# First layernorm: the second batch's tiles are split in rows and turned by DMA transposes

## The chip, the cores and the metric

The kernel runs on one core of one Trainium2 chip. The time is that of the whole program on the device, in microseconds (us). A core has five engines, each with its own instruction queue: TensorE (PE, matrix products), VectorE (DVE), ScalarE (ACT), GpSimd (POOL) and SyncE (SP). SP computes nothing here; it issues every DMA of this kernel. Work on different engines is ordered by semaphores alone: an instruction waits until a counter has reached a value, and everything behind it on the same engine waits with it.

## The reference

One decoder layer on x of 2 batches x 512 rows x 1024 columns, in float32:

```
x = x + attention(layernorm(x))      # 32 query heads, 8 key/value heads of 128, causal
x = x + fake_quant(layernorm(x)) @ fake_quant(ctx)
x = x + gated_ffn(layernorm(x))      # 64 experts of rank 8, the best 16

# the head of attention(h), with h = layernorm(x):
q  = h @ Wq.T                        # 4096 columns
kc = h @ Wk_down.T ; vc = h @ Wv_down.T      # 256 columns each: the latents
k, v = (split of [kc, vc]) @ Wk_up.T, Wv_up.T
```

The change is in the first layernorm, at the very start, and in the latents' product behind it.

## The kernel before, in words

Every float32 operand of a product is split in two float16 parts, a high part (ACT rounds it) and a low part (DVE takes the rest, line 1188), and a product is three passes: high x high, high x low, low x high (line 1672).

The 1024 rows of x are eight tiles of 128 rows: tiles 0 to 3 are batch 0, tiles 4 to 7 are batch 1. `QT` is 4 and `TT` is 8. For each tile the opening does this:

- DVE takes mean and variance (line 1196), POOL a power (line 677), DVE the scale and the bias (lines 1210 to 1218), in `ln_stats` and `ln1_rstd`.
- ACT writes the normed rows, float32, to `hn`, which lies in the tensor `prob` (line 890, `ln1_apply`). `hn` has two places; tile t takes place t % 2.
- PE turns the tile, since the products need the columns of x on the partitions: eight 128x128 float32 transposes into two PSUM banks (line 1686, `columns`).
- ACT writes the high part from PSUM (`columns_hi`, two instructions of 128x512), DVE the low part (`columns_lo`, two instructions), into `h_block(b, j)`: the right factors of the query products, for batch b and half j of the columns. Three of these four blocks lie in `h_b`. The fourth, batch 1 and half 0, lies in `wo_in`.

Semaphores here: `ln_done` counts tiles normed, `ln_turned` half tiles turned, `ht_hi` and `ht_lo` split instructions of ACT and DVE.

The latents' product follows in four pairs of tiles ("pair" in the code: pair 0 is tiles 0 and 1, up to pair 3 with tiles 6 and 7). Each pair has four parts hp = 0 to 3, of 24 matmuls 128x256 each, 96 in all. PE's order puts the turning of tiles 2 to 7 between these parts, one tile ahead of the first two parts of pairs 0, 1 and 2. A pair waits for the low parts of its tiles. After pair 1 (batch 0) and pair 3 (batch 1) the latents go through ACT (line 882) and DVE (line 1240) into `lat`, which lies in `o_t`. Then PE computes keys and values of seven key/value heads (`kv_products`), 30 matmuls for each head and batch, whose results ACT and DVE split and SP stores to memory (`kv_parts`).

Beside this, POOL forms sums of the blocks (`part_sums`, line 701), four chunks of ten instructions on `q_tmp`, for the fast scheme of the query products. Its first chunk starts when all eight tiles are split. ACT and DVE take these sums out of `q_tmp` (`t_split`) behind the second head's keys and values, and POOL starts a second chunk only then.

SP's queue at the start is: loads of x and of weights, the first chunk of the context (`load_chunk`), then the loop with the loads of `up` weights (line 601, each waits for `up_lo`) and the stores of keys and values (line 607). Elsewhere in the kernel SP already issues DMA transposes: `turn` for the attention weights (128x1280, lines 554 and 557), and at the end `turn_h3` (128x1024, lines 636 and 638) and `turn_gated` (128x512, lines 644 and 646).

Of the kernel before, what the change touches and what calls it, by code (L numbers as in the profile page):

```python
# [8 lines left out]
F16 = mybir.dt.float16  # L9
BF16 = mybir.dt.bfloat16  # L10

P = 128
BATCH, SEQ, DIM = 2, 512, 1024
TOK = BATCH * SEQ
TT = TOK // P
# [181 lines left out]
    return LAST_WO + 2 * WO_STEP + max(c for c in range(WO_CHUNKS) if PAIR1_BANK[c % 8] == bank) + 1  # L197


def kind_of(g):  # L200
    if not isinstance(g, int):
        return "mid"
    return {0: "first", KV_HEADS - 1: "last"}.get(g, "mid")
# [7 lines left out]
def decoder_layer(nc, x, ctx_in, wq, wdown, wup, wo, a_w, b_w, router_w, keys, quant, ctx_whole, b_whole, kv_whole, out):  # L211
# [8 lines left out]
    with ctx:  # L220
# [74 lines left out]
              v_sb[:, :, :, :, :].rearrange("p a b c d -> p (a b c d)").bitcast(F32))  # L295
        h3_t = wq_sb[:, :, :, :].rearrange("p a b c -> p (a b c)").rearrange("p (t m n) -> p t m n", t=2, m=2)
        gated = q_tmp[:, 0, :]
        h3_s = wo_in[:, :, :].rearrange("p a b -> p (a b)").bitcast(F16).rearrange("p (t m n) -> p t m n", t=2, m=2)
        z_s = prob_s[:, :, 0:2 * HALF].rearrange("p t (m n) -> p t m n", m=2)
        column_term = wq_in[:, :, :].rearrange("p a b -> p (a b)").rearrange("p (b n) -> p b n", b=BATCH)  # L300
# [50 lines left out]
        o_lo = sem("o_lo")  # L351

        ht_hi = sem("ht_hi")
        wq_hi = sem("wq_hi")
        wo_hi = sem("wo_hi")
        up_hi = sem("up_hi")
# [83 lines left out]
        def _(sp):  # L440
# [154 lines left out]
                        load_ctx(0)  # L595

            load_chunk(0, 0)
            for n in range(KV_HEADS - 1):
                if n + 3 < KV_HEADS:
                    sp.wait_ge(up_lo, n + 1)  # L600
                    sp.dma_start(up_in[:, n % 3, :], wup[KV_ORDER[n + 3]]).then_inc(up_loaded[n % 3], 16)
                if n == 4:
                    for place in range(4):
                        sp.wait_ge(wq_lo, place + 1)
                        load_wq(place, 2 + place // 2)
                sp.wait_ge(gen_read, 2 * DOWN + 4 * (n + 1))
                sp.dma_start(kv_whole[KV_ORDER[n]], kv_stage[:, n % 2, :, :, :].rearrange("p a b c -> p (a b c)"))\
                    .then_inc(kv_stored[n % 2], 16)
# [54 lines left out]
        def _(pool):  # L663
# [36 lines left out]
                    at = q_tmp[:, place, :]  # L700
                    nc.gpsimd.tensor_tensor(at, at if left_ is None else left_, right, op).then_inc(t_op, 1)

            pool.wait_ge(ht_lo, 2 * TT)
            for n in range(KT // 2):
                part_sums(n)

# [98 lines left out]
        def _(act):  # L805
# [63 lines left out]


            def columns_hi(t):
                for j in range(2):
                    act.wait_ge(ln_turned, 2 * t + j + 1)
                    split_hi(h_block(t // QT, j)[:, 0, :, t % QT * P:(t % QT + 1) * P],
                             ps[:, 2 * (t % 2) + j, :].rearrange("p (k n) -> p k n", k=4), ht_hi, S_H)
# [7 lines left out]
                ins.then_inc(gen_hi, 1)  # L883

            def ln1_apply(t):
                if t >= 2:

                    act.wait_ge(ln_turned, 2 * (t - 1))
                act.wait_ge(rstd_done, t + 1)
                nc.scalar.activation(hn[:, t % 2, :], x_sb[:, t, :], ACT.Identity, bias=ln_bias[:, t:t + 1],  # L890
                                     scale=rstd1[:, 2, t:t + 1]).then_inc(ln_done, 1)
# [287 lines left out]
        def _(dve):  # L1179
# [47 lines left out]
            nc.vector.tensor_copy(ident_b[:, :], ident[:, :]).then_inc(newton, 1)  # L1227
            newtons[0] += 1
            def columns_lo(t):
                for j in range(2):  # L1230
                    dve.wait_ge(ht_hi, 2 * t + j + 1)
                    hi, lo = (h_block(t // QT, j)[:, part, :, t % QT * P:(t % QT + 1) * P] for part in range(2))
                    split_lo(lo, ps[:, 2 * (t % 2) + j, :].rearrange("p (k n) -> p k n", k=4), hi, ht_lo, S_H)
# [430 lines left out]
        def _(pe):  # L1664
# [27 lines left out]
            for pair in range(PAIRS):  # L1692
# [1 line left out]
                b, part = pair // 2, pair % 2  # L1694
                at = part * 2 * P
                for hp in range(DOWN):
                    if hp < 2 and 2 * pair + 2 + hp < TT:
                        columns(2 * pair + 2 + hp)
                    if hp == 0:
                        pe.wait_ge(ht_lo, 4 * (pair + 1))  # L1700
                    if pair == 0:
                        pe.wait_ge(wo_lo, hp + 1)
                    if b == 1 and part == 0:
# [31 lines left out]
                    pe.wait_ge(gen_read, max(kv_before(v), 2 * DOWN if b == 1 else DOWN))  # L1735
                    (k_product if kind == "k" else v_product)(n, b, kv_bank(v)).then_inc(gen_done, 1)

            pe.wait_ge(ht_lo, 2 * TT)
            for n in range(KV_HEADS - 1):
                kv_products(n)  # L1740
            for n in range(PLAIN_Q):
# [323 lines left out]
```

## Time and profile before

| | |
|---|---|
| time, median of 3 runs | 1109.15 us (1106.42 to 1109.94) |
| the profiled execution: time, span | 1110.08 us, 1108.3 us |
| granted TensorE clock, mean | 0.989 of full |
| PE busy | 1064.9 us, 96% of the span |
| DVE busy | 905.2 us, 82% |
| ACT busy | 530.3 us, 48% |
| POOL busy | 411.6 us, 37% |
| chain that ended last | PE 85%, DVE 8%, ACT 3%, issue 2%, DMA 1%, POOL 1% |
| DMA transposes in the program | 162, all issued by SP |

The span counts from the first to the last instruction, and the execution's own time is 1.8 us more. "Busy" counts an engine's instructions; it doesn't tell on what the end depends. The chain of waits does: it goes back from the last instruction to what released each step. In the row of the granted clock 1.00 is TensorE's full clock (2.4 GHz) and 0.50 the half (1.2 GHz).

### The profile page before, as it was taken

Reading aid. Unit: us, or ns where it says so; the run is one execution under the profiler, and the core shown is the slowest. Engines: PE = TensorE matmul, PEld = TensorE weight load, DVE = VectorE, ACT = ScalarE, POOL = GpSimd, SP = SyncE. Lnnn points to the kernel's source line nnn. Section 1 sums busy time; section 2 is a strip of 40 time slices with the busy share of each in tenths; the row PEclk is TensorE's granted clock in tenths of the full one; section 3 lists DMA queues with packets and bytes.
Section 4 is the critical chain, followed back from the end, with each engine's and each line's share of the span. In section 5 each row is a group of like instructions: output and inputs, shape, how many; then the busy total and the mean of one; then the engine's idle time right before and its main releaser. Section 6 shows DMA issues by size and latency. Waiting matters only on the chain.

```text
span 1108.3 us, 19648 instructions
## 1 busy us (share of the span) xinstructions
PE 1064.9 (96%) x6229; PEld 568.7 (51%) x6236; DVE 905.2 (82%) x1861; ACT 530.3 (48%) x1081; POOL 411.6 (37%) x423
## 2 busy tenths in 40 slices
PE   4999998999999999999999999999999998969998
PEld 3876544555555555555555555555555554434443
DVE  6789578988787978787888888787978798888973
ACT  4646366555454445454544455454545453233420
POOL 2049755534353434343442434353434243000000
PEclk8999999999999999999999999999999999989999
DMA  8016145654544445454545554554445378224442
GB/s 315 1 58 257 77 88 136 164 117 110 139 123 114 106 123 136 110 132 116 139 100 124 132 117 112 132 123 114 106 126 136 83 187 230 101 43 82 102 99 86
DMA packets 229601, 135.74 MB, mean 122 GB/s; under 512 B 200112, under 2 KB 202288, under 8 KB 228656
## 3 DMA queue, kind: packets, MB, share of 16 engines
q1 hardware_dynamic: 229552, 135.11, 48.1%
q8 instruction: 27, 0.44, 0.2%
q14 instruction: 22, 0.18, 0.1%
HBM read 68.23 MB, written 17.83 MB: 78 GB/s over the span
## 4 chain that ended last, share of the span: by engine, by line
PE 85%; DVE 8%; ACT 3%; issue 2%; DMA 1%; POOL 1%; SPq 0%; DVEq 0%; ACTq 0%; POOLq 0%
PE ps L1672 81%; PE ps L1924 2%; ACT prob L1034 1%; DVE wo_sb L1188 1%; DVE h_b L1188 1%; DVE prob L1397 1%; PE ps L1995 1%; DMA wq_sb<-wo_in 1%; DVE prob_t L1188 1%; DMA o_t<-in_wdown 1%; PE ps L1686 0%; ACT prob L890 0%; DVE stats L1196 0%; ACT wo_sb L807 0%; DVE wq_sb L1188 0%
## 5 line engine op out<-in xcount | busy, mean ns | idle before, releaser
L771 POOL TENSOR_SCALAR prob<-prob,row_inv 128x128 f32<-128x128 f32 (+3 forms) x256 | 203.5, 815 | 438.0 <-DVE row_inv L1368 438.0
L1672 PE MATMUL ps<-wo_sb,o_t 128*128 128x512 f16 x1536 | 353.0, 380 | 3.6 <-DVE x_sb L1379 3.6
L1672 PE MATMUL ps<-h_b,wq_sb 128*128 128x512 f16 x1524 | 344.9, 381 | 0.0
L1034 ACT ACTIVATE prob<-prob,neg_max 128x128 f32<-128x128 f32 (+3 forms) x256 | 140.6, 550 | 220.8 <-DVE neg_max L1403 220.8
L1672 PEld LDWEIGHTS ps<-h_b,wq_sb 128*128 128x128 f16 x1524 | 148.4, 98 | 178.2 <-issue 4.4
L1672 PEld LDWEIGHTS ps<-wo_sb,o_t 128*128 128x128 f16 x1536 | 147.6, 98 | 173.1 <-DVE x_sb L1379 6.3
L1379 DVE SCALAR_TENSOR_TENSOR x_sb<-ps,x_sb 128x512 f32<-128x512 f32 x256 | 174.2, 686 | 54.8 <-PE ps L1672 53.9
L1672 PE MATMUL ps<-prob_t,v_sb 128*128 128x128 f16 (+2 forms) x960 | 116.6, 274 | 6.5 <-DMA prob_t<-prob_s 6.5
L1672 PE MATMUL ps<-k_t,q_t 128*128 128x512 f16 (+3 forms) x768 | 114.8, 299 | 0.6 <-DVE neg_max L1403 0.5
L1397 DVE CUSTOM_DVE_ANT_0 prob<-ps,mask 128x512 f32<-128x512 f32 (+3 forms) x256 | 110.3, 484 | 2.3 <-issue 1.6
L1672 PEld LDWEIGHTS ps<-prob_t,v_sb 128*128 128x128 f16 x960 | 83.5, 98 | 36.8 <-DMA prob_t<-prob_s 7.3
L807 ACT ACTIVATE q_t<-q_tmp 128x512 f16<-128x512 f32 x60 | 37.8, 630 | 131.8 <-DVE q_tmp L1355 131.8
L1355 DVE SCALAR_TENSOR_TENSOR q_tmp<-ps,q_tmp 128x512 f32<-128x512 f32 x105 | 72.1, 686 | 29.8 <-PE ps L1672 27.4
L1188 DVE SCALAR_TENSOR_TENSOR prob_s<-prob,prob_s 128x1280 f16<-128x1280 f32 x64 | 95.0, 1484 | 0.1
L807 ACT ACTIVATE prob_s<-prob 128x1280 f16<-128x1280 f32 x64 | 80.6, 1259 | 28.0 <-POOL prob L771 27.3
L1672 PEld LDWEIGHTS ps<-k_t,q_t 128*128 128x128 f16 x768 | 66.9, 98 | 51.7 <-issue 1.0
L1188 DVE SCALAR_TENSOR_TENSOR wq_sb<-wq_in,wq_sb 128x512 f16<-128x512 f32 x94 | 67.5, 732 | 0.5 <-ACT wq_sb L807 0.3
L1188 DVE SCALAR_TENSOR_TENSOR q_t<-q_tmp,q_t 128x512 f16<-128x512 f32 x60 | 61.7, 1049 | 0.7 <-ACT q_t L807 0.7
L1188 DVE SCALAR_TENSOR_TENSOR o_t<-ps,o_t 128x512 f16<-128x512 f32 x64 | 44.3, 692 | 20.1 <-ACT o_t L807 20.1
L801 POOL TENSOR_TENSOR rstd<-var_eps,minus_half 128x1 f32<-128x1 f32 x16 | 8.8, 549 | 139.0 <-DVE var_eps L1202 139.0
L807 ACT ACTIVATE wq_sb<-wq_in 128x512 f16<-128x512 f32 x94 | 56.5, 618 | 3.0 <-POOL wq_in L730 3.0
L1034 ACT ACTIVATION_READ_ACCUMULATOR prob<-prob,neg_max 128x1 f32 x256 | 47.8, 187 | 0.0
(146 smaller groups left out, 1138.4 us busy)
## 6 DMA issues: line engine op xcount, KB each, us to landing
wq_in<-in_wq SPq DMA_DIRECT2D x64, 256.0 KB, 3.5
wo_in<-in_wo SPq DMA_DIRECT2D x32, 512.0 KB, 3.9
side_in<-in_ctx SPq DMA_DIRECT2D x16, 512.0 KB, 4.3
kv_parts<-wo_sb SPq DMA_DIRECT2D x7, 1024.0 KB, 5.0
x_sb<-in_x SPq DMA_DIRECT2D x8, 512.0 KB, 9.2
ctx_quantised<-side_out SPq DMA_DIRECT2D x16, 256.0 KB, 2.9
h_b<-ctx_quantised SPq DMA_DIRECT2D x2, 2048.0 KB, 10.8
out<-x_sb SPq DMA_DIRECT2D x8, 512.0 KB, 2.9
```

The costliest lines, as they stand in the source:

```text
L771: ins = nc.gpsimd.tensor_scalar(at, at, row_inv[:, u % 2, q:q + 1], S_P, ALU.mult, ALU.mult)
L801: nc.gpsimd.tensor_tensor(rstd0[:, k * TT + t:k * TT + t + 1], var_eps[:, k * TT + t:k * TT + t + 1], minus_half[:, :], ALU.pow).then_inc( ...
L807: nc.scalar.activation(dst, src, ACT.Copy, scale=scale).then_inc(signal, 1)
L1034: ins = nc.scalar.activation(at, at, ACT.Exp, bias=neg_max[:, n % 2, q:q + 1], scale=SOFTMAX, accum_out=row_sum[:, n % 2, q:q + 1])
L1188: nc.vector.scalar_tensor_tensor(dst, src, scale, hi, ALU.mult, ALU.subtract).then_inc(signal, 1)
L1355: nc.vector.scalar_tensor_tensor(q_tmp[:, dst, :], ps[:, Q_BANK[product % 2], :], Q_OUT, q_tmp[:, src, :], ALU.mult, ALU.add).then_inc(com ...
L1379: nc.vector.scalar_tensor_tensor(at, ps[:, bank, :], WO_OUT, at, ALU.mult, ALU.add).then_inc(wo_read, 1)
L1397: ins = nc.vector.tensor_tensor_reduce(prob[:, u % 2, at:at + width], ps[:, at // HALF, at % HALF:at % HALF + width], mask[:, SEQ - width: ...
L1672: ins = nc.tensor.matmul(out_, lhs(i), rhs(j), start=start and n == 0, stop=stop and n == 3 * len(pairs) - 1)
L1924: ins = nc.tensor.matmul(ps[:, x_banks(t)[j], :], x_qt[:, t % 2, k * P:(k + 1) * P], ctx_q[:, b, k, j * HALF:(j + 1) * HALF], start=k == 0 ...
L1995: ins = nc.tensor.matmul(ps[0:2 * ROUTER, SMALL_BANK, R_COL:R_COL + P], router_sb[:, k, :, :].rearrange("p a r -> p (a r)"), h3_t[:, t % 2 ...
```

## The change

Tiles 0 to 3 stay as they were. Tiles 4 to 7 are no longer turned by PE. ACT and DVE split the normed rows as they stand in `hn` into `h_s`, a float16 view of `q_tmp` with two places of a high and a low row block (one instruction of 128x1024 on each engine for a tile). SP then turns each part by two DMA transposes of 128x512, one for each half of the columns, directly into `h_block(1, j)`. Two new semaphores `h_landed`, one for each place, count the landings; a tile has four.

Who waits for them: PE before pair 2 and before pair 3, in place of `ht_lo`; ACT before it splits tiles 6 and 7, as their places in `h_s` must be free; POOL before its first sum, since it writes `q_tmp` and reads the blocks. ACT's norming of tiles 6 and 7 now waits for the splits of tiles 4 and 5 instead of their turning. PE's wait for `ht_lo` ahead of `kv_products` is gone.

```diff
+def h_splits(t):
+    return 2 * t + 2 if t < QT else QT + t + 1
...
+        h_s = q_tmp[:, :, :].rearrange("p a b -> p (a b)").bitcast(F16).rearrange("p (t m n) -> p t m n", t=2, m=2)
...
             load_chunk(0, 0)
+            for t in range(QT, TT):
+                for part, split in enumerate((ht_hi, ht_lo)):
+                    sp.wait_ge(split, h_splits(t))
+                    for j in range(2):
+                        sp.dma_start_transpose(h_block(1, j)[:, part, :, t % QT * P:(t % QT + 1) * P],
+                                               h_s[:, t % 2, part, j * HALF:(j + 1) * HALF]).then_inc(h_landed[t % 2], 16)
             for n in range(KV_HEADS - 1):
...
-            pool.wait_ge(ht_lo, 2 * TT)
+            pool.wait_ge(ht_lo, 2 * QT)
+            for n in range(2):
+                pool.wait_ge(h_landed[n], 64 * (QT // 2))
...
             def columns_hi(t):
+                if t >= QT:
+                    act.wait_ge(ln_done, t + 1)
+                    if t >= QT + 2:
+                        act.wait_ge(h_landed[t % 2], 64)
+                    split_hi(h_s[:, t % 2, 0, :], hn[:, t % 2, :], ht_hi, S_H)
+                    return
...
             def ln1_apply(t):
-                if t >= 2:
+                if 2 <= t < QT + 2:
                     act.wait_ge(ln_turned, 2 * (t - 1))
+                if t >= QT + 2:
+                    act.wait_ge(ht_hi, h_splits(t - 2))
+                    act.wait_ge(ht_lo, h_splits(t - 2))
...
             def columns_lo(t):
+                if t >= QT:
+                    dve.wait_ge(ht_hi, h_splits(t))
+                    split_lo(h_s[:, t % 2, 1, :], hn[:, t % 2, :], h_s[:, t % 2, 0, :], ht_lo, S_H)
+                    return
...
-                    if hp < 2 and 2 * pair + 2 + hp < TT:
+                    if hp < 2 and pair == 0:
                         columns(2 * pair + 2 + hp)
-                    if hp == 0:
+                    if hp == 0 and b == 0:
                         pe.wait_ge(ht_lo, 4 * (pair + 1))
+                    if hp == 0 and b == 1:
+                        for n in range(2):
+                            pe.wait_ge(h_landed[n], 64 * (part + 1))
...
-            pe.wait_ge(ht_lo, 2 * TT)
```

On PE, around the end of pair 1 and the start of pair 2 (`ident,prob` is the turning of a tile, `h_b,wo_sb` and `wo_in,wo_sb` are products of the latents), the program before has this:

```order
L1672 MATMUL ps<-h_b,wo_sb 128x256 x72
L1686 MATMUL ps<-ident,prob 128x128 [waits ht_lo,ln_done]
L1686 MATMUL ps<-ident,prob 128x128 x3
L1686 MATMUL ps<-ident,prob 128x128 [waits ht_lo]
L1686 MATMUL ps<-ident,prob 128x128 x3
L1672 MATMUL ps<-wo_in,wo_sb 128x256 [waits gen_read,ht_lo]
L1672 MATMUL ps<-wo_in,wo_sb 128x256 x11
L1672 MATMUL ps<-h_b,wo_sb 128x256 x12
```

And the changed program has this at the same place:

```order
L1701 MATMUL ps<-h_b,wo_sb 128x256 [waits ht_lo]
L1701 MATMUL ps<-h_b,wo_sb 128x256 x95
L1701 MATMUL ps<-wo_in,wo_sb 128x256 [waits gen_read,h_landed1,h_landed0]
L1701 MATMUL ps<-wo_in,wo_sb 128x256 x11
L1701 MATMUL ps<-h_b,wo_sb 128x256 x12
```

The 32 transposes of tiles 4 to 7 are gone from PE (8 ahead of each of the first two parts of pairs 1 and 2), pair 1 runs through as 96 matmuls, and the first matmul of pair 2 waits for the DMAs' landings. The first of pair 3 has the same wait.

On SP, behind the first loads, the program before goes from the context's first chunk straight to the loop of `up` loads and key/value stores:

```order
L457 DMA wq_in<-in_wq 128x512 x4
L498 DMA side_in<-in_ctx 128x1024
L601 DMA prob_t<-in_wup 128x512 [waits up_lo]
L607 DMA kv_parts<-wo_sb 128x4096 [waits gen_read]
L601 DMA prob_t<-in_wup 128x512 [waits up_lo]
```

The changed program has sixteen DMA transposes in between, of which the last four (tile 7) and what follows are:

```order
L609 DMA_TRANSPOSE wo_in<-q_tmp 128x4x128 [waits ht_hi]
L609 DMA_TRANSPOSE h_b<-q_tmp 128x4x128
L609 DMA_TRANSPOSE wo_in<-q_tmp 128x4x128 [waits ht_lo]
L609 DMA_TRANSPOSE h_b<-q_tmp 128x4x128
L614 DMA prob_t<-in_wup 128x512 [waits up_lo]
L620 DMA kv_parts<-wo_sb 128x4096 [waits gen_read]
```

Each tile is four transposes in the order high, high, low, low, one tile behind the other in one queue, and the `up` load stands behind all of them.

## Rows read from the trace of the kernel before

**Rows 1.** Chain of waits, 0 to 140 us: start us, us, what

```profile
34.58 0.87 PE ps L1686 x8
...
46.81 0.87 PE ps L1686 x8
47.68 2.62 PE ps L1672 x24
50.30 0.87 PE ps L1686 x8
51.17 18.35 PE ps L1672 x168
...
72.92 8.09 PE ps L1672 x90
...
104.14 30.11 PE ps L1672 x192
```

**Rows 2.** Timeline, 36 to 57 us: start us, us, engine, line, operation

```profile
36.50 0.58 ACT L807 ACTIVATE wo_in<-ps 128x512 f16<-128x512 f32 x1
...
37.72 0.68 DVE L1188 SCALAR_TENSOR_TENSOR h_b<-ps,h_b 128x512 f16<-128x512 f32 x1
...
42.40 0.59 ACT L807 ACTIVATE h_b<-ps 128x512 f16<-128x512 f32 x1
...
44.28 0.68 DVE L1188 SCALAR_TENSOR_TENSOR h_b<-ps,h_b 128x512 f16<-128x512 f32 x1
...
51.61 0.60 ACT L807 ACTIVATE wo_in<-ps 128x512 f16<-128x512 f32 x1
...
53.06 0.62 ACT L807 ACTIVATE h_b<-ps 128x512 f16<-128x512 f32 x1
...
55.56 0.68 DVE L1188 SCALAR_TENSOR_TENSOR h_b<-ps,h_b 128x512 f16<-128x512 f32 x1
```

**Rows 3.** Timeline: a weight's split of 128x1024 from SBUF

```profile
29.43 1.04 ACT L807 ACTIVATE wo_sb<-o_t 128x1024 f16<-128x1024 f32 x1
...
30.50 1.23 DVE L1188 SCALAR_TENSOR_TENSOR wo_sb<-o_t,wo_sb 128x1024 f16<-128x1024 f32 x1 [2.31 <-ACT wo_sb L807]
```

**Rows 4.** Groups on q_t: the issues of 128x512 transposes, ns min/median/max

```profile
L644 SPq DMA_TRANSPOSE q_t<-prob_s x7: 1202/1218/1269, 992.8 to 1084.9; - x7
L646 SPq DMA_TRANSPOSE q_t<-prob_s x7: 1265/1267/1270, 994.1 to 1086.1; - x7
```

**Rows 5.** DMA issues by line: count, median us from issue to landing

```profile
q_t<-prob_s SPq DMA_TRANSPOSE x14, 2.5
```

**Rows 6.** Timeline of SP's queue near the end

```profile
1038.71 1.21 SPq L644 DMA_TRANSPOSE q_t<-prob_s  x1
1039.97 1.27 SPq L646 DMA_TRANSPOSE q_t<-prob_s  x1
...
1068.15 2.31 SPq L638 DMA_TRANSPOSE wq_sb<-wo_in  x1
```

**Rows 7.** Timeline of PE behind three gaps; the gap stands in brackets

```profile
170.64 3.14 PE L1672 MATMUL ps<-prob_t,v_sb 128*128 128x128 f16 x15 [2.96 <-DMA prob_t<-prob_s]
...
984.37 0.43 PE L2007 MATMUL ps<-keys_sb,mask 32*128 32x64 f32 x2 [2.49 <-ACT mask L1116]
...
994.81 1.89 PE L1995 MATMUL ps<-wq_sb,router_sb 128*32 128x128 f16 x16 [3.60 <-DMA wq_sb<-wo_in]
```

**Rows 8.** Three stretches: busy PE, PEld, DVE, ACT, POOL; granted clock, DMA share, GB/s

```profile
171.00:174.00 3.00, 3.00 (x14) 1.69 (x12) 2.16 (x4) 1.41 (x3) 3.00 (x3) 0.50 0.66 225
...
984.40:991.00 6.60, 6.28 (x29) 2.84 (x30) 5.49 (x24) 4.10 (x7) 0.55 (x1) 1.00 0.24 47
...
995.00:1000.00 5.00, 5.00 (x24) 2.62 (x23) 4.70 (x13) 1.19 (x3) 1.00 (x2) 0.50 0.74 82
```

**Rows 9.** Timeline: the split behind which POOL's second chunk starts

```profile
82.04 1.14 ACT L807 ACTIVATE h_b<-q_tmp 128x512 f16<-128x512 f32 x2
...
83.70 1.47 POOL L701 TENSOR_TENSOR q_tmp<-wo_in,h_b 128x512 f32<-128x512 f16 x1 [14.09 <-DVE h_b L1188]
```

More of the change, by code:

```diff
@@ L353, in decoder_layer @@
         ht_hi = sem("ht_hi")
+        h_landed = [sem(f"h_landed{n}") for n in range(2)]
         wq_hi = sem("wq_hi")
```

## The prediction

> **What bounds the kernel now.** I read the page's table of busy shares first: PE is busy 96% of the span, so a change gains only where it shortens PE's own work or a stretch in which PE waits. Then I read the chain of waits over the first 140 us, where the change lies [rows 1]. From about 32 us to 69.5 us it is PE alone: products of the latents, with four pieces of turning between them, 0.87 us each (the rows at 34.58, 46.81 and 50.30 and one more at 38.07). It ends at 51.17 + 18.35 = 69.52 us, goes over the latents' splits on ACT and DVE, and PE goes on at 72.92. Of what follows, one property matters: keys and values start from PE's end in that stretch, and nothing there has a clock of its own. So the question is when the product of pair 3 ends. Next I read the timeline for when each tile's parts are split [rows 2, 3], then the rows on DMA transposes further on in the program [rows 4 to 6], as the opening has none, and last PE's gaps with the clock behind them [rows 7, 8].
>
> **What goes.** Four pieces of 0.87 us leave PE, 3.48 us. That is the whole of what the change could give on the path. Two of them lie ahead of pair 1's end, which moves from 46.81 to 46.81 - 1.74 = 45.07 us. ACT and DVE save nothing to speak of: two splits of 128x512 from PSUM (0.58 and 0.68 us each [rows 2]) become one of 128x1024 from SBUF, 1.04 on ACT and 1.23 on DVE [rows 3]. What is lost is the overlap: DVE could begin on the first half while ACT did the second, and now waits for the whole.
>
> **When the tiles are split.** Tile 4: ACT starts at 36.50 as before (it came from its own norming, not from PE), is done at 37.54, and DVE at about 38.8, where it was 37.72 + 0.68 = 38.40. This 0.4 us is handed on: DVE computes the scale of tile 6 behind it, and ACT norms with that. Tile 5: high part before at 42.40 + 0.59 = 42.99, now about 43.4; low part before at 44.28 + 0.68 = 44.96, now about 45.4. Tiles 6 and 7: ACT started at 51.61, now at about 52.1 (between them lie the latents of batch 0). The high parts are ready at 53.1 and 54.1, the low parts at about 55.4 and 56.6 (before, tile 7's was ready at 55.56 + 0.68 = 56.24). The wait for free places in the row block costs nothing by this: tile 5 lands long before 53 us.
>
> **What SP's queue makes of it.** This is the term that decides. A transpose of 128x512 holds SP for 1.22 to 1.27 us [rows 4], from one start to the next it is 1.26 us [rows 6], with a check of a semaphore between two parts some 1.31; I take 1.29. From its issue to its landing it is 2.5 us [rows 5]; I take 2.55. A tile has four of them, 5.2 us of queue, whatever the sizes of its data. Tile 5: the four issues start at 43.5, 44.8, 46.1 and 47.3, the last lands at 49.9. Tile 6 and 7 come together, eight issues from 53.15 on: the last starts at 53.15 + 7 x 1.29 = 62.2 and lands at 64.7 us. Each low part is ready before its turn, so it is the queue, not DVE, that sets this. The bounds of the unmeasured pitch in this place: 1.21 (the shortest issue) gives 64.2; 1.35 (an allowance of 0.06 over mine for the strided destination) gives 65.2; one long issue of 2.31 us in the eight, as at 1068.15 [rows 6], adds 1.0. It is one of ten of 1.7 us or more among the trace's 162 transposes.
>
> **On PE.** A pair is 96 matmuls of 18.35 / 168 = 0.109 us, 10.49 us. Pair 1 ends at 45.07; pair 2 waits for tile 5 until 49.9, 4.8 us of idleness, and would end at 60.4. Pair 3 waits for tile 7 until 64.75 and ends at 75.24 us. Before it was 69.52. The difference is +5.7 us.
>
> **The clock.** Behind PE's gaps of 2.96 and 3.60 us the granted clock is 0.50, the half level of 1.2 GHz, through stretches of 3.0 and 5.0 us; behind the gap of 2.49 us it is 1.00 [rows 7, 8]. The gap of 4.8 us ahead of pair 2 is longer than both that lost it, so I count on the half clock there, which adds half of such a stretch, 1.5 to 2.5 us, to pair 2. But pair 2 has 4.3 us to spare ahead of pair 3, so this costs nothing: it only shortens the second gap to 1.8 to 2.8 us. The nearest row, 2.49, kept its clock, so I take the full clock for pair 3 and keep the loss of it, +1.5 to +2.5, for the range. The Trainium skill speaks of this too ("TensorE: Matmul & The Clock Gate", section "Why this matters for your kernels": gaps between bursts of matmuls put the engine back to the half rate); the trace agrees on two gaps of the three. It speaks against the change, as the turning on PE that is taken out was also what kept the engine at work.
>
> **Further on.** POOL's first chunk of sums waits for the landings, from 56.3 us to 64.7. It took 13 us before and has to be done when ACT takes the first sums at 82.04, which itself moves to about 87.8; its second chunk starts behind that split [rows 9] and moves with it. So 8.4 us more of waiting are covered by the 14.09 us for which POOL stood idle. The `up` load behind the sixteen transposes is issued at about 63.5 instead of 57 us, for weights of the fourth head, which are split some 20 us later. The stores behind it move with the products. A shift of the chain at 69.5 goes through the 90 matmuls at 72.92, the stretch that DVE paces, and the 192 at 104.14 [rows 1] without being taken up: DVE works there on what PE hands it and waits for it at first. I value what follows at nothing.
>
> **The sum.** -3.48 for the turning, +4.8 and +4.3 for the two waits, +0.05 for the starts: +5.7 us. The profiled execution took 1110.08 us and would take 1115.8. It is 0.9 above the median of 1109.15, so I forecast 1115.0 us, 0.5% more. A measurement of this kernel tells about 0.3%, 3.3 us, from no change.
>
> **Rivals.**
> 1. *Pair 3 loses the clock too, or a long issue falls among the last eight.* All as above, plus 1.5 to 2.5 or plus 1.0: 1116 to 1118. For it: the gaps lie close together in length (2.49 kept, 2.96 lost) and I compute up to 2.8, and 4.3 if pair 2 kept its clock. Chance 0.23.
> 2. *The queue is not the limit.* If issues overlapped with the data's way, a tile would land 2.5 us behind its low part: tile 5 at 47.9, tile 7 at 59.15. Pair 2 would end at 58.4, pair 3 at 59.2 + 10.49 = 69.7, +0.2 us: 1109.4. In the Trainium skill's words ("Advanced Engine Details and Errata", section "X-Bar Transpose (TRN2)") transposing DMAs "are as fast as regular DMAs", with 350 to 400 GB/s expected; by that figure the eight transposes of 131 KB take, as an estimate, under 3 us, and this would be the outcome. The rows speak against it: the issue alone takes 1.2 us whether the next one is ready or not, in every one of the 162. Chance 0.07.
> 3. *The delay is taken up later.* DVE paces the stretch from 81 to 104 us; if some of its work there could run ahead in the longer wait, up to 3 us came back: 1112. Against it: in that stretch it splits what PE has just written, and POOL, which slows it, starts by its signal. Chance 0.07.
> 4. *Faster.* If both waits for tiles were hidden, the 3.48 us would remain: 1105.7. The point from which this decides is a landing of tile 7 before 45.07 + 10.49 = 55.6 us. Its low part is not even split until 56.6. Only an ACT and DVE order that moved earlier could do this, and it isn't changed. Chance 0.03.
>
> **How the numbers follow.** The forecast has 0.60, from 1113.5 to 1116.5 by the bounds of pitch and of the run. The range from 1111.5 to 1118 takes in the first rival and part of the third, and leaves out the second and the fourth, with some noise, 2 in 10. Slower by over 0.3% means above 1112.5: the forecast and the first rival, less what noise of the two medians takes away, 0.83. Within 0.3%: the second, the third and that part, 0.14. Faster 0.03.
>
> **What would show it.** In the changed profile: no float32 turning on PE behind the fourth tile; sixteen transposes in SP's queue from about 37.6 to 63.5 us, the last eight without a gap at 1.25 to 1.31 us; a PE wait of 4 to 5 us for a DMA ahead of the first product with the block in `wo_in`, and a second one of 1.8 to 4.5 us 96 matmuls later; half clock between them; pair 3's end near 75.2; POOL's first sum near 64.8, and its second chunk released by DVE as before. If the second wait is missing, or the transposes follow each other faster than 1.2 us, the queue's term is wrong; if both are there and the time is the same as before, it is the step on what follows.

## The result: slower by 0.5 to 0.7%, as forecast

| | kernel before | changed kernel | ratio (95% interval) |
|---|---|---|---|
| first comparison, 6 and 6 runs | 1108.84 us (1106.42 to 1110.43) | 1117.41 us (1113.72 to 1118.43) | 1.007 (1.0049 to 1.0092) |
| same kernels on another chip, 18 and 7 runs | 1108.62 us (1106.53 to 1113.04) | 1114.69 us (1113.28 to 1116.53) | 1.0048 (1.0031 to 1.0065) |
| profiled execution, time and span | 1110.08, 1108.3 | 1113.72, 1111.9 | |
| busy share of PE, DVE, ACT, POOL in it | 96%, 82%, 48%, 37% | 96%, 81%, 48%, 37% | |

The forecast was 1115.0 us. By the first row the change costs 7.8 us (5.4 to 10.2), by the second, with more runs, 5.3 us (0.31 to 0.65% of 1108.62: 3.4 to 7.2 us). The step worked out on the path was 5.7, which lies in both intervals. The two overlap, and whether more than noise sets them 2.5 us apart was not tested. (The ratio is not that of the two medians, which lie 8.6 and 6.1 us apart.) The profiled execution is the fastest of its six, and why it shows only 3.6 us is told below.

The chain of waits of the changed kernel over the first 150 us (start us, us, what; SPq is SP's queue issuing). The rows that answer to [rows 1]:

```profile
60.66 1.26 SPq L609
61.97 2.48 DMA h_b<-q_tmp
64.59 10.65 PE ps L1701 x96
...
78.63 8.09 PE ps L1701 x90
...
109.85 30.11 PE ps L1701 x192
```

Where the chain before ran over PE alone from about 32 to 69.5 us, it now runs through SP's queue: issue behind issue, then the last one's landing, then pair 3. The 90 matmuls start at 78.63 instead of 72.92 and the 192 at 109.85 instead of 104.14. Both are 5.71 us late; between the two nothing is added and nothing given back.

One thing in these 5.71 us is not the change's. The first weights landed earlier in this execution, and ACT's norming of tile 4, whose code is the same, began at 27.97 us instead of 28.28. In the two chains, before and changed:

```profile
1.66 6.04 DMA o_t<-in_wdown
...
28.28 1.24 ACT prob L890
```

```profile
1.66 5.73 DMA o_t<-in_wdown
...
27.97 1.24 ACT prob L915
```

Counted from that norming, the 90 matmuls start 6.0 us later than before (50.66 against 44.64).

The timeline of PE (start us, us, engine, line, operation, in brackets the idle time before it and its releaser):

```profile
31.47 13.47 PE L1701 MATMUL ps<-h_b,wo_sb 128*128 128x256 f16 x120 [0.37 <-DVE wo_sb L1213]
49.89 2.72 PE L1701 MATMUL ps<-wo_in,wo_sb 128*128 128x256 f16 x12 [4.95 <-issue]
52.41 2.76 PE L1701 MATMUL ps<-h_b,wo_sb 128*128 128x256 f16 x12
...
61.57 1.47 PE L1701 MATMUL ps<-h_b,wo_sb 128*128 128x256 f16 x12
64.59 1.47 PE L1701 MATMUL ps<-wo_in,wo_sb 128*128 128x256 f16 x12 [1.54 <-DMA h_b<-q_tmp]
```

Pair 1 ends at 31.47 + 13.47 = 44.94 us. Then come the two waits: 4.95 us ahead of pair 2 and 1.54 us ahead of pair 3. Between them twelve matmuls take 2.72 us at first and 1.47 later on (each group of twelve starts 1.31 us behind the last at full clock), so pair 2 ends at 63.05 and not at 49.89 + 10.49. The releaser of the first wait is given as "issue": the profile has nothing for it, but the landings of tile 5 end then (next block).

SP's queue, of the sixteen transposes the first of each group and the last, and what follows:

```profile
37.25 1.31 SPq L609 DMA_TRANSPOSE wo_in<-q_tmp  x1
...
43.09 1.57 SPq L609 DMA_TRANSPOSE wo_in<-q_tmp  x1
...
47.32 1.27 SPq L609 DMA_TRANSPOSE h_b<-q_tmp  x1
52.89 1.19 SPq L609 DMA_TRANSPOSE wo_in<-q_tmp  x1
...
61.97 1.27 SPq L609 DMA_TRANSPOSE h_b<-q_tmp  x1
63.28 0.58 SPq L614 DMA_DIRECT2D prob_t<-in_wup  x1
```

Tiles 6 and 7 are eight issues, 52.89 to 61.97: (61.97 - 52.89) / 7 = 1.30 us from start to start, with no gap. With the landing, 2.5 us behind its issue, tile 5 is there at 49.8 and tile 7 at 64.5, which are the two points at which PE goes on.

The stretches by granted clock (length us; busy PE, PEld, DVE, ACT, POOL; granted clock, DMA share, GB/s):

```profile
50.00:54.00 4.00, 4.00 (x20) 2.74 (x19) 3.83 (x10) 3.92 (x8) 0.00 (x0) 0.50 0.01 2
...
60.00:65.00 5.00, 3.46 (x32) 2.89 (x31) 0.00 (x0) 0.00 (x0) 0.38 (x1) 1.00 0.49 86
65.00:70.00 5.00, 5.00 (x48) 4.47 (x47) 0.91 (x3) 1.51 (x4) 4.69 (x5) 1.00 0.13 49
```

The clock is at the lower level, 1.2 GHz, behind the gap of 4.95 us, and stays at the full 2.4 GHz behind the one of 1.54. While the queue sets the pace (60 to 65 us), the DMA engines are busy half of the time at 86 GB/s: what is scarce is issuing, not bandwidth, as experiment 1 shows. ACT and DVE have nothing left to do there.

**Why the profile shows 3.6 us.** Starts in the changed trace less starts of the same code before: +5.71 us at the 192 matmuls, +6.33 at the end of the first head and at 921 us, then +4.64. The 1.69 between lie in one group of matmuls. Before:

```profile
927.68 7.04 PE L1672 MATMUL ps<-wo_sb,o_t 128*128 128x512 f16 x24 [2.42 <-DVE x_sb L1379]
```

and in the changed kernel, at the same place with the same gap ahead, and again at the place of [rows 7]'s third row:

```profile
934.00 5.35 PE L1701 MATMUL ps<-wo_sb,o_t 128*128 128x512 f16 x24 [2.42 <-DVE x_sb L1408]
...
999.45 1.07 PE L2026 MATMUL ps<-wq_sb,router_sb 128*32 128x128 f16 x16 [3.40 <-DMA wq_sb<-wo_in]
```

Behind the first of these gaps the clock fell before and held in this execution: 7.04 - 5.35 = 1.69 us. Behind the second it fell in both, but here only after the sixteen matmuls of the row (0.66 granted from 999 to 1004 us, against 0.50 in [rows 8]): from this row to the next of its kind it is 17.07 us and was 18.04, which gives back 1.0 us more. 6.33 - 1.69 - 1.0 = 3.6, the difference of the spans. The repeated profile of the changed kernel shows that this comes and goes in one and the same kernel:

```profile
933.91 7.04 PE L1701 MATMUL ps<-wo_sb,o_t 128*128 128x512 f16 x24 [2.42 <-DVE x_sb L1408]
```

Its span is 1114.7 us, 6.4 above before. Over the eleven traces of this study these 24 matmuls took 7.04 us four times and 5.35 seven times, each time behind 2.41 or 2.42 us of idleness. There are two more such places; the last section adds them up.

### The profile page after: what moved, and what is told of

It reads as the page before. It is cut to its first block, busy times and chain, and to the rows that moved or that the text cites. A ratio compares the mean times of both kernels' runs of the same rounds, so it can differ in the third digit from the quotient of the medians.

```text
span 1111.9 us, 19592 instructions
## 1 busy us (share of the span) xinstructions
PE 1063.1 (96%) x6197; PEld 565.4 (51%) x6204; DVE 902.3 (81%) x1857; ACT 530.3 (48%) x1077; POOL 410.4 (37%) x423
## 4 chain that ended last, share of the span: by engine, by line
PE 82%; DVE 9%; ACT 4%; issue 2%; DMA 2%; POOL 1%; SPq 1%; ACTq 0%; DVEq 0%; POOLq 0%
PE ps L1701 79%; PE ps L1955 2%; ACT prob L1059 1%; DVE h_b L1213 1%; DVE wo_sb L1213 1%; DVE prob L1426 1%; ACT prob L915 1%; DVE o_t L1269 1%; PE ps L2026 1%; DMA wq_sb<-wo_in 1%; DVE prob_t L1213 1%; DVE stats L1221 1%; DMA o_t<-in_wdown 1%; SPq L609 0%; DVE q_tmp L1213 0%
## 5 line engine op out<-in xcount | busy, mean ns | idle before, releaser
L1059 ACT ACTIVATION_READ_ACCUMULATOR prob<-prob,neg_max 128x1 f32 x256 | 47.8, 187 | 0.0
```

Of the source, the lines that this page charges most:

```text
L1059: ins = nc.scalar.activation(at, at, ACT.Exp, bias=neg_max[:, n % 2, q:q + 1], scale=SOFTMAX, accum_out=row_sum[:, n % 2, q:q + 1])
```

## Experiments

Here "the key start" is the start of the 90 matmuls in the chain: 72.92 us before, 78.63 changed. It is a sharper measure than the time, but it moves with the first loads: ACT's norming of tile 4 began between 27.78 and 28.77 us in these traces. So the table also counts the key start from that norming.

| trace | tile 4's norming | key start | from norming, less before's 44.64 |
|---|---|---|---|
| before | 28.28 | 72.92 | |
| changed, and again (8) | 27.97, 27.98 | 78.63, 78.64 | +6.0, +6.0 |
| 1, twice the transposes | 27.80 | 96.94 | +24.5 |
| 2, half the transposes | 28.42 | 77.34 | +4.3 |
| 3, no wait | 28.11 | 72.52 | -0.2 |
| 4, clock kept up | 27.78 | 79.15 | +6.7 |
| 5, only tiles 4 and 5 | 28.14 | 77.03 | +4.3 |
| 6, only tiles 6 and 7 | 28.77 | 81.71 | +8.3 |
| 7, half, split early | 28.21 | 73.84 | +1.0 |
| 9, the same, gap filled | 28.10 | 72.08 | -0.7 |

Diffs are against the changed kernel, and the counts in the waits, which change with the number of transposes, are left out of them. Where only one time is given, there was one run; 18 runs of the kernel before lie 6.5 us apart, so the starts carry the reading there and not the time. Each kernel has one trace, the changed one two.

**1. Twice the transposes.** Each of 128x256 instead of 128x512, eight a tile, the same bytes.

```diff
-                    for j in range(2):
-                        sp.dma_start_transpose(h_block(1, j)[:, part, :, ...], h_s[:, t % 2, part, j * HALF:...])
+                    for c in range(4):
+                        sp.dma_start_transpose(h_block(1, c // 2)[:, part, 2 * (c % 2):2 * (c % 2) + 2, ...],
+                                               h_s[:, t % 2, part, c * 2 * P:(c + 1) * 2 * P])
```

> The changed kernel with each tile's transposes cut in two: eight of 128x256 a tile instead of four of 128x512, the same bytes. Theory (SP's issue of about 1.26 us per transpose sets the landing, whatever its size): tile 5's eight issues begin at 42.5 us behind tile 4's and the last lands near 60 us; tile 7's last issue starts at about 42.5 + 23 x 1.28 = 72 us or, if each starts late, up to 74, and lands near 74.5; pair 3 starts there instead of 64.6, about 10 us later, and the time rises by 9 to 10 us. Rival (the data's way through the DMA engines sets it, issues overlap): the same bytes take the same time, pair 3 starts within 1 us of 64.6 and the time stays.

Measured: 1134.35 us, one run. The issues by group (ns min/median/max, first and last start us), and PE's timeline:

```profile
L609 SPq DMA_TRANSPOSE wo_in<-q_tmp x16: 1226/1246/1662, 37.1 to 75.0; - x16
```

```profile
59.31 2.72 PE L1701 MATMUL ps<-wo_in,wo_sb 128*128 128x256 f16 x12 [14.53 <-issue]
...
80.09 2.71 PE L1701 MATMUL ps<-wo_in,wo_sb 128*128 128x256 f16 x12 [8.86 <-DMA h_b<-q_tmp]
```

Half the data takes the same 1.25 us of the queue. The key start moves by 18.3 us to 96.94, more than expected, because the expectation counted its issues wrongly: there are 32, without a gap from 37.1 to 78.9 us, not 24 from 42.5 (tile 4's own eight take until 47.8). Pair 3 starts 15.5 us later (80.09 against 64.59) and loses the clock behind 8.86 us of waiting, another 2.8. The queue's term stands, and rival 2 (a limit by bytes) is out: by bytes nothing would have moved.

**2. Half the transposes.** High and low parts side by side in the row block, so that one transpose of 128x1024 takes both. The view `h_s` and the two splits into it are changed to match (left out here).

```diff
-                for part, split in enumerate((ht_hi, ht_lo)):
-                    sp.wait_ge(split, h_splits(t))
-                    for j in range(2):
-                        sp.dma_start_transpose(...)
+                sp.wait_ge(ht_lo, h_splits(t))
+                for j in range(2):
+                    sp.dma_start_transpose(h_block(1, j)[:, :, :, ...].rearrange("p m k n -> p (m k) n"),
+                                           h_s[:, t % 2, j, :, :].rearrange("p m n -> p (m n)"))
```

> The changed kernel with half the transposes: high and low part of a half tile lie side by side, and one transpose of 128x1024 takes both, so two a tile, both behind the low part. Theory (issues set it): tile 5 lands at 45.0 + 1.3 + 3.2 = 49.5 us, nearly as before; tile 7's low part is ready at 56.3, behind it two issues and 3.2 us from the last issue to landing, 62.2. Pair 2, with the half clock behind the first gap, ends only at 63.0, so the second wait is gone and pair 3 starts 1.5 us earlier than in the changed kernel, at 63.0; time 1.5 us below the changed kernel. Rival (bytes set it): landing stays at 64.5 and so does the time.

Measured: 1112.62 us (1109.05 to 1116.47, 8 runs), 1.0045 of before (1.0025 to 1.0065).

```profile
L608 SPq DMA_TRANSPOSE h_b<-q_tmp x4: 1318/1327/1341, 40.4 to 59.7; - x4
```

```profile
50.02 2.72 PE L1700 MATMUL ps<-wo_in,wo_sb 128*128 128x256 f16 x12 [4.62 <-issue]
...
63.30 1.47 PE L1700 MATMUL ps<-wo_in,wo_sb 128*128 128x256 f16 x12
```

Twice the data costs the queue 5% more (1327 against 1267 ns) and lands 3.2 instead of 2.5 us behind the issue. The second wait is gone, but pair 3 starts only 1.3 us earlier (63.30; 1.7 by the norming), since pair 2 itself is late and at half clock for a little more than its first quarter. The key start is 77.34. With the queue out of the way, the first wait remains: tile 5's low part is split at about 45, and a transpose has yet to be issued and land.

**3. No wait at all.** Batch 1's latents read the blocks of batch 0.

```diff
-                    if hp == 0 and b == 1:
-                        for n in range(2):
-                            pe.wait_ge(h_landed[n], 64 * (part + 1))
...
-                                          lambda j, k=k: h_block(b, k // 4)[:, j, k % 4, at:at + 2 * P])
+                                          lambda j, k=k: h_block(0, k // 4)[:, j, k % 4, at:at + 2 * P])
```

> The changed kernel, in which the latents of batch 1 are computed from batch 0's blocks (this part of the result is other than the reference's), so that PE does not wait for any landing. All DMA transposes, splits and POOL's wait stay. Theory: pair 2's first part starts at 45.0 us, but its parts 1 to 3 wait for batch 0's latents to leave PSUM (about 50.4, 52.2 and 53.9 us), so pair 3 ends near 68.8 us instead of 75.1: 6.3 us below the changed kernel and 0.7 below the kernel before, 1108. So of the 3.48 us of turning taken off PE only 0.7 could ever be had without the waits. Rival (the time is added elsewhere, by POOL's late first sum or by the DMA traffic): pair 3 ends early but the time stays above the kernel before by 2 us or more.

Measured: 1108.67 us (1105.98 to 1112.97, 10 runs), 1.0003 of before (0.9986 to 1.0021).

```profile
50.60 18.51 PE L1701 MATMUL ps<-h_b,wo_sb 128*128 128x256 f16 x168 [2.88 <-DVE o_t L1269]
```

The key start is 72.52: 6.1 us ahead of the changed kernel, and only 0.4 ahead of before (0.2 by the norming). So the two waits and what hangs on them are the whole loss, and the turning that left PE is worth at most 0.4 us here and not 3.48. With PE's work gone it stood 2.88 us for DVE, which had the latents of batch 0 to split before their banks came free. My "that is the whole of what the change could give" was an upper bound, and far above what there was to be had in this order of ACT's and DVE's work. That decides rival 4. With the splits moved earlier the best was 0.8 us (experiment 9).

**4. The clock kept up.** 44 and 36 extra matmuls into a bank about to be overwritten, in the places of the two waits.

```diff
                     if hp == 0 and b == 1:
+                        for n in range((44, 36)[part]):
+                            nc.tensor.matmul(ps[:, 0, 0:2 * P], wo_sb[:, 0, 0, 0:P], h_block(0, 0)[:, 0, 0, 0:2 * P],
+                                             start=True, stop=True)
```

> The changed kernel with 44 extra matmuls of 128x256 ahead of pair 2 and 36 ahead of pair 3, into a PSUM bank that nobody reads, which fill the two gaps (4.8 and about 4.1 us). Theory (the half clock behind the first gap costs pair 2 2.7 us, but that is hidden in the wait for tile 7): the clock stays at 1.00, pair 2 ends at 60.4, pair 3 starts at 64.6 as before and ends at 75.1; no change within 0.3 us at the start of keys and values (78.6). Rival (the clock is what costs): keys and values start 2 us or more earlier.

Measured: 1112.36 us, one run. PE's timeline and the stretch at the start of pair 2:

```profile
44.59 4.97 PE L1732 MATMUL ps<-h_b,wo_sb 128*128 128x256 f16 x44
49.62 1.47 PE L1701 MATMUL ps<-wo_in,wo_sb 128*128 128x256 f16 x12
...
65.11 1.47 PE L1701 MATMUL ps<-wo_in,wo_sb 128*128 128x256 f16 x12 [0.93 <-DMA h_b<-q_tmp]
```

```profile
50.00:55.00 5.00, 5.00 (x48) 4.48 (x47) 4.83 (x11) 4.92 (x10) 0.00 (x0) 1.00 0.14 28
```

The clock stays full and pair 2 ends at 60.1 instead of 63.05, and it does not help: pair 3 still starts with tile 7's landing, and the key start is 79.15. The 2.67 us that the half clock cost pair 2 were free, as the prediction had it. That the key start is 0.5 us later, where 0.3 was allowed, is one long issue among the last eight, which the prediction had priced at 1.0:

```profile
56.54 1.98 SPq L609 DMA_TRANSPOSE h_b<-q_tmp  x1
```

The span of 1110.6 is not a gain of the filling: it is 4 us shorter than the repeated profile's (1114.7), though the key start is later; here the 24 matmuls near 930 us kept their clock, and so did the stretch near 1000 us.

**5 and 6. One half of the change each.** Tiles 4 and 5 by DMA and 6 and 7 on PE, or the other way round. The edit writes the counts of the semaphores as functions of a list, and the list is the experiment:

```diff
+DMA_TILES = (4, 5)        # and (6, 7)
...
-            for t in range(QT, TT):
+            for t in DMA_TILES:
```

> Only tiles 4 and 5 go through DMA transposes; tiles 6 and 7 are turned by PE between the parts of pair 2, as in the kernel before. Theory (each of the two waits alone is enough to lose nearly all): pair 2 starts at 49.9 us behind tile 5's landing, loses the clock at its start (+2.7 us as in the changed kernel), holds two turnings of 0.87 us and ends near 64.9; pair 3 follows at once and ends near 75.3, keys and values start near 78.8, within 0.4 us of the changed kernel. If the clock's fall were free here too, they would start at 76.1. Rival (only the second wait, for tile 7, counts): keys and values start as in the kernel before, 72.9.

> Only tiles 6 and 7 go through DMA transposes; tiles 4 and 5 are turned by PE between the parts of pair 1, as in the kernel before. Theory (the queue's eight issues from 53 us set pair 3's start): pair 2 starts at about 46.9 us with no wait, ends near 57.4, then a gap of 7 us; tile 7 lands at 64.5 as in the changed kernel, pair 3 starts there, at half clock for 3 to 5 us (plus 1.7 to 2.7), and keys and values start near 80.5. Rival (the queue is late only because tiles 4 and 5 went through it first): tile 7 lands earlier than 64, and keys and values start 2 us or more before those of the changed kernel.

Measured: 1110.42 us for tiles 4 and 5, 1118.86 us for 6 and 7, one run each. PE of the first:

```profile
49.96 2.25 PE L1714 MATMUL ps<-wo_in,wo_sb 128*128 128x256 f16 x12 [3.98 <-issue]
```

and of the second, in pair 3, with SP's queue and the clock of the stretch:

```profile
64.98 2.72 PE L1714 MATMUL ps<-wo_in,wo_sb 128*128 128x256 f16 x12 [6.22 <-DMA h_b<-q_tmp]
```

```profile
53.15 1.31 SPq L622 DMA_TRANSPOSE wo_in<-q_tmp  x1
...
62.35 1.27 SPq L622 DMA_TRANSPOSE h_b<-q_tmp  x1
```

```profile
65.00:70.00 5.00, 5.00 (x24) 3.46 (x25) 0.00 (x0) 0.00 (x0) 4.68 (x5) 0.50 0.16 52
```

The key starts are 77.03 (+4.1 on before) and 81.71 (+8.8); both expectations missed. The first is neither the 78.8 of the theory nor the 72.9 of the rival: one of the two turnings (0.87 us) fell into the wait at 44.95, where it cost nothing, and the clock cost 1.7 us, not 2.7. In the second, 80.5 was expected, and the clock cost 2.9 us (13.35 for the product of pair 3) where at most 2.7 had been allowed. Tile 7 lands as late without tiles 4 and 5 ahead of it in the queue (last issue 62.35), so its lateness is its own eight issues from 53.15 on. And this half of the change costs more than the whole: with pair 2 on time the wait ahead of pair 3 grows to 6.22 us and the clock falls on the path, where the whole change had the fall in pair 2, under cover. The losses of the halves do not add up.

**7. Shorter queue and earlier splits.** Experiment 2, and ACT and DVE split tiles 5 to 7 ahead of most latents of batch 0. The edit of ACT's order (DVE's is the same):

```diff
             for t in range(TT):
-                if t in (5, 6):
-                    for hp in down_heads(t):
-                        latent_hi(0, hp)
+                if t == 7:
+                    latent_hi(0, 1)
                 columns_hi(t)
+                if t == 5:
+                    latent_hi(0, 0)
+                if t == 7:
+                    latent_hi(0, 2)
+                    latent_hi(0, 3)
```

> Two transposes of 128x1024 a tile, and ACT and DVE split tiles 5, 6 and 7 ahead of batch 0's latents where they can: tile 5 before part 0 of the latents, tile 6 before part 1, tile 7 before parts 2 and 3. Nothing is left out. Theory (it is all in when the last landing comes): tile 5's low part is ready at 42.8 and lands at 47.3; pair 2 starts there behind a gap of 2.3 us, at full clock, and ends near 57.8; tile 7 lands near 55, so pair 3 follows at once and ends near 68.3; keys and values start at 71.6, 7.0 us before the changed kernel and 1.3 before the kernel before; the time is 1107, which is no measurable difference to the kernel before. If the gap of 2.3 us loses the clock, 1.5 to 2.5 us more. Rival (something else in the changed kernel costs, beyond the two waits): keys and values start early but the time stays above the kernel before by 2 us or more.

Measured: 1108.66 us (1105.53 to 1111.09, 12 runs), 0.9995 of before (0.9981 to 1.0008).

```profile
47.65 1.76 PE L1708 MATMUL ps<-wo_in,wo_sb 128*128 128x256 f16 x12 [2.46 <-DMA h_b<-q_tmp]
49.20 2.77 PE L1708 MATMUL ps<-h_b,wo_sb 128*128 128x256 f16 x12
```

The second wait is gone and the first halved, and yet the key start is 73.84 where 71.6 was expected, or 1.5 to 2.5 us more if the clock fell. It fell, behind a gap of 2.46 us, a hair less than the 2.49 that kept it in [rows 7].

**8. The changed kernel again.** Unchanged.

> The changed kernel again, for a narrower interval. Theory (the shift at the start of keys and values, 5.7 us, plus 0.6 in the first head's softmax, is all there is): 6.3 us over the kernel before, ratio 1.0057. Rival (something later in the program adds to it, as the first six runs' medians, 8.6 us apart, would have it): ratio 1.0075 or more.

Measured: 1114.69 us, 1.0048 of before (1.0031 to 1.0065), which holds the theory's 1.0057 and leaves out the rival's 1.0075. The key start is 78.64, 0.01 us from the first trace's, as the norming of tile 4 happened to start together too.

**9. Experiment 7 with the gap filled.** Twenty extra matmuls ahead of pair 2.

```diff
+                        for n in range((20, 0)[part]):
+                            nc.tensor.matmul(ps[:, 0, 0:2 * P], wo_sb[:, 0, 0, 0:P], h_block(0, 0)[:, 0, 0, 0:2 * P], ...)
```

> The kernel with two transposes of 128x1024 a tile and early splits, in which the clock fell behind a gap of 2.46 us (pair 2 began at 47.65 and pair 3 at 59.95, where full clock would have given 58.14), with 20 extra matmuls of 128x256 (2.2 us, into a PSUM bank that nobody reads) in that gap. Nothing is left out. Theory (that gap's half clock was the last thing that kept it above the kernel before): the clock stays at 1.00, pair 3 starts at 58.1, keys and values at 72.0, 0.9 us before the kernel before; the time is 0 to 1 us below the kernel before, which is no measurable difference, ratio 0.999. Rival (the clock's fall has a cause other than the gap): 0.50 appears between 45 and 55 us all the same and keys and values start at 73.8 again.

Measured: 1109.32 us (1105.93 to 1111.41, 12 runs), 1.0000 of before (0.9988 to 1.0012).

```profile
44.92 2.35 PE L1739 MATMUL ps<-h_b,wo_sb 128*128 128x256 f16 x20
47.55 1.47 PE L1708 MATMUL ps<-wo_in,wo_sb 128*128 128x256 f16 x12 [0.29 <-issue]
```

The clock stays full and the key start is 72.08, as expected and 0.84 ahead of before. The time doesn't show it: against before, 2.05 us are lost again in the first head, between 105 and 195 us. No version measurably beats the kernel before.

**What happens in the first head.** Between the key start and the head's end (193.10 us before) experiments 1, 2, 7 and 9 lose 2.0 to 2.1 us against the kernel before, the others 0.1 to 0.7. The difference is the clock behind PE's last wait in that head. From that wait's end to the end of the head it is 11.69 to 11.77 us in those four traces, and 10.10 in the seven others, before included. Experiment 2, where it fell (0.63 granted over the next 4 us), and experiment 4, where it stayed at 1.00:

```profile
187.85 2.40 PE L1700 MATMUL ps<-prob_t,v_sb 128*128 128x128 f16 x15 [2.22 <-DMA prob_t<-prob_s]
190.05 6.47 PE L1700 MATMUL ps<-h_b,wq_sb 128*128 128x512 f16 x24
```

```profile
189.69 1.81 PE L1701 MATMUL ps<-prob_t,v_sb 128*128 128x128 f16 x15 [2.26 <-DMA prob_t<-prob_s]
191.34 5.34 PE L1701 MATMUL ps<-h_b,wq_sb 128*128 128x512 f16 x24
```

What is left without it, 0.4 to 0.5 us, is in the range of the others. What stays open is why the clock fell at that place in all three kernels with merged transposes (and in experiment 1, which has none): with one trace of each, chance isn't excluded.

## Why the prediction was right, step by step

- **What goes.** 3.48 us left PE; pair 1 ended at 44.94, forecast 45.07. As an amount of work that was right; as what the change could at best give it was not (0.4 us, experiment 3).
- **When tiles are split.** The single splits of 128x1024 cost what [rows 3] said:

```profile
36.18 1.04 ACT L822 ACTIVATE q_tmp<-prob 128x1024 f16<-128x1024 f32 x1
37.25 1.22 DVE L1213 SCALAR_TENSOR_TENSOR q_tmp<-prob,q_tmp 128x1024 f16<-128x1024 f32 x1 [0.69 <-ACT q_tmp L822]
```

  All of it began 0.3 us earlier than I had it: the first split at 36.18 and not 36.50, tile 5's queue at 43.09 and not 43.5, tile 6's at 52.89 and not 53.15. That is the earlier landing of the first weights (0.31 us), which no forecast could know.
- **The queue.** 1.29 us a transpose was forecast, 1.30 measured; landing 2.55 and 2.5. One issue of 1.57 and none of 2.31 among the sixteen; in experiments 3 and 4 one of 2.10 and one of 1.98 fell among the last eight, so the term for a long issue was rightly kept. The price by the piece is shown by the doubling of experiment 1. The Trainium skill ("Advanced Engine Details and Errata", section "X-Bar Transpose (TRN2)") says that such transposes are as fast as regular DMAs; no run here measures the rate of the bytes alone, and in this kernel it is not the bytes that set the time. "DMA: Bandwidth & Descriptors", section "Rules for kernel authors", of the same skill asks that many small transfers be put together into a large one, and experiments 1 and 2 agree: 1.25, 1.27 and 1.33 us of queue for 128x256, 128x512 and 128x1024.
- **The two waits.** 4.8 forecast, 4.95 measured; the second at 1.8 to 2.8 with the clock lost in pair 2, 1.54 measured. It is shorter since the half clock took 13.16 - 10.49 = 2.67 us, above the 2.5 that I had as the end. Pair 3 started at 64.59, forecast 64.75. Its end in the chain, 64.59 + 10.65 = 75.24, is the forecast's to the digit, and that is luck: it started 0.16 us early, and the chain counts a lone row of 96 matmuls 0.16 us longer than my 10.49.
- **The clock.** Lost behind 4.95, kept behind 1.54, as taken. That the loss in pair 2 costs nothing is shown by experiment 4. What rival 1 would have looked like is shown by experiment 6: 13.35 us for the product of pair 3.
- **Further on.** "I value what follows at nothing" held over the keys and values (5.71 at both ends), and POOL had the room it was given:

```profile
64.62 1.15 POOL L714 TENSOR_TENSOR q_tmp<-wo_in,h_b 128x512 f32<-128x512 f16 x1 [23.18 <-DMA h_b<-q_tmp]
...
89.42 1.47 POOL L714 TENSOR_TENSOR q_tmp<-wo_in,h_b 128x512 f32<-128x512 f16 x1 [12.53 <-DVE h_b L1213]
```

  The second chunk moved from 83.70 [rows 9] to 89.42, by 5.72, released by DVE as before. What I didn't see is the first head, which adds 0.6 us (5.71 becomes 6.33): PE waits 2.20 us for a row maximum at 172.25, where it had waited 0.53 at 165.90, and gets back 1.04 at the transfer before (0.41 at 157.19 for 1.45 at 152.52). Why was not tested.
- **The sum.** +5.7 forecast, +5.71 at the key start (+6.0 by the norming), in time 7.8 us (5.4 to 10.2) and 5.3 us (3.4 to 7.2). The agreement of the key start to 0.01 us is again partly luck, as 0.3 us of it are the first load's. The profiled execution was to be 1115.8 and was 1113.72: 2.7 us less for the clock at 934 and 999 us, which I took to be fixed, and 0.6 more for the first head.

The rivals: the second fell with experiment 1, the fourth with experiment 3, the third by the trace (no delay was taken up up to 921 us). The first didn't happen in either trace of the changed kernel, and by [rows 7] alone could not have been excluded.

## What to carry to other kernels

Moving work off the busiest engine pays only if the replacement arrives by the time the engine would be free: look first for who gates it next (here DVE, which left 0.4 of 3.48 us, and 0.8 with its work put in another order) and for when the new path delivers. DMA transposes within the core were priced by the piece in the issuing queue here, about 1.3 us each from 128x256 to 128x1024, so make few large ones, and count the issues between the last split and its reader. Where two waits lie in a row, a loss of clock in the first stretch can be free under the second wait, and halving the change can bring it onto the path.

## What was not expected of the hardware

- **Gaps of 2 to 3.6 us of PE may or may not lose the clock, at one place and in one length.** The same 24 matmuls behind the same 2.42 us took 7.04 us in four traces and 5.35 in seven. Elsewhere it fell behind 1.96, 2.22 and 2.46 us and held behind 2.88 (experiment 3, ahead of pair 2) and, in the same experiment, behind 2.95:

```profile
170.90 1.81 PE L1701 MATMUL ps<-prob_t,v_sb 128*128 128x128 f16 x15 [2.95 <-DMA prob_t<-prob_s]
```

  Here 15 matmuls took 1.81 us where they took 3.14 behind 2.96 in [rows 7]. At this place it fell behind 2.95 us in experiments 6 and 7 and held behind 2.95 in experiment 5 and 2.97 in experiment 4. Even the 3.60 of [rows 7], from which the prediction read a loss, was not certain to lose it. At its place experiment 2 kept the clock and the repeated changed kernel lost it:

```profile
999.63 1.07 PE L2025 MATMUL ps<-wq_sb,router_sb 128*32 128x128 f16 x16 [3.54 <-DMA wq_sb<-wo_in]
```

```profile
1001.08 1.89 PE L2026 MATMUL ps<-wq_sb,router_sb 128*32 128x128 f16 x16 [3.55 <-DMA wq_sb<-wo_in]
```

  Ahead of the latents' pairs the gaps of 3.98, 4.62, 4.95, 5.03, 6.22, 8.86 and 14.53 us all lost it. A single gap of 2 to 3.6 us can't be forecast from its length by these traces.
- **Three such places are nearly all that sets these traces apart behind the key start.** The last wait of the first head cost 1.6 to 1.7 us where the clock fell (experiments 1, 2, 7, 9). The 24 matmuls near 930 us cost 1.7 (before, 6, 8, 9). Near 1000 us, from the row above to the next of its kind, it is 15.38 us where the clock held (2, 3, 4, 5, 7), 17.07 in the changed kernel's first trace and 17.93 to 18.12 in the others, up to 2.7 more. From the key start to the end of the span, in code that is the same, the eleven traces take 1031.4 to 1037.5 us; with these three taken off, 1031.0 to 1031.7. That the scatter of a kernel's other runs has the same cause is likely, but they have no traces. One time can't tell 2 us; the starts in the trace can, to the 1 us by which the first loads move them, and better when counted from a start ahead of the change.
- **Issue time barely knows the size**: 1.25, 1.27 and 1.33 us for 64, 128 and 256 KB, while the landing grows from 2.4 to 2.5 and 3.2 us.
